# Row maxima of the fifth query tile over 320 and 320 keys instead of 512 and 128

## The chip, the cores and the metric

The kernel runs on one core of a Trainium2 chip. The metric is the device time of one execution in microseconds (us). A profile of one execution goes with it. It names the engines so: PE is TensorE's matmuls, PEld its weight loads, DVE is VectorE, ACT is ScalarE, POOL is GpSimd, SP is the queue that issues the transfers.

## What is computed

One layer of a transformer on x of shape (4, 1024, 128), in float32: causal attention with 16 heads of width 64, a residual and a layer norm, then a feed-forward part (128 to 512, a butterfly of nine stages, GELU, a second butterfly, 512 to 128), a residual and a layer norm. What the change touches is the maximum inside the softmax:

```python
q_BSHK = jnp.einsum('BSE,EHK->BSHK', x_BSE, w_q)
k_BMHK = jnp.einsum('BSE,EHK->BSHK', x_BSE, w_k)
logits_BSHM = jnp.einsum('BSHK,BMHK->BSHM', q_BSHK, k_BMHK) / math.sqrt(Kq)
mask = jnp.where(qpos >= mpos, 0.0, -jnp.inf)[None, :, None, :]
probs_BSHM = jax.nn.softmax(logits_BSHM + mask, axis=3)
```

## The kernel before

The attention runs in 32 units, one for each of 4 batches and 8 pairs of heads. The 1024 queries of a unit are 8 tiles of 128, in two chunks of 512 (`CH`; `TPC` is 4 tiles a chunk, and the index `qt == TPC` is the fifth tile). A unit has twelve steps (`STEPS`, line 47): step s takes one key tile against one chunk of queries. Chunk 0 has steps 0 to 3 and chunk 1 steps 4 to 11. Of each step `scores` (L718) makes the logits for head 0 and head 1 of the pair, two matmuls each (L727, L733), transposed, keys on the partitions, into one of two PSUM banks `SC`. ScalarE makes the exponential of each (L906) into `PR`. There are only two `SC` banks, so a half can start only when the exponential of the half two before has been made: this is the wait in L726. GpSimd masks (L534) and adds up the exponentials (L549), and the attention matmuls (L754) take them from `PR`, most of them in blocks behind steps 1, 8 and 9 (`PV_AFTER`). Before the block behind step 8 VectorE must have scaled the unit before (L1121), and for that the inverse sums must have been broadcast by a chain of DMAs (L443, L446, L449).

The exponentials are taken of logits less their row's maximum. The maxima of unit u + 1 are found while unit u runs: TensorE makes the logits once more, this time with the queries on the partitions (L666), and VectorE takes the maximum along the row. A row of query tile qt has up to (qt + 1) x 128 keys. It is cut in two parts (`keys_of`, L352). Part 0 is the first 512 keys, part 1 the rest, so the fifth tile has 512 and 128 keys. Where a part ends on the diagonal, VectorE adds the causal mask `CMASK` and takes the maximum in one custom instruction (L1034, with a short one behind it that reads the accumulator). Where it doesn't, a plain reduction does it (L1037). Each part writes its cell of `MP`.

This work is cut in groups. A group fills one of the four PSUM banks `WORK`, in turn, and its bank must have been emptied by the consumer of the group four before (`take_work`, L618). `MAXES` (line 79) is the list of the groups of maxima, 21 a unit. Groups 0 and 1 hold two tiles each. Group 6 holds two pieces of 128 keys: part 1 of the fifth tile for both heads. Groups 7 and 8 are part 0 of the fifth tile, 512 keys, one for each head. `FILL` (line 86) says by hand where each group stands in TensorE's order, for each step at three places: between the scores of head 0 and head 1, behind the scores of head 1, and late, behind the attention matmuls where there are any. ScalarE and VectorE consume in the same order. In step 5 group 6 stands between the halves, and groups 7 and 8 stand late; in step 6 groups 9 and 10 stand late, and nothing else. `FIRST_FILL` (line 133) is the same for unit 0, in which also the maxima of unit 0 itself (`FIRST`) are placed, and `PREFETCH` (line 170) is what comes ahead of it. VectorE's `window` (L1123) sets two other pieces of work behind certain groups: the low halves of the weights behind group 0, and those of the value weights behind group 6.

The other fillers are the projections of queries and keys (L637 to L639), those of the values (L647 to L649), the sums of the exponentials (L714) and the output projection (L679).

Of the kernel before, what the change touches and what calls it, by code (L numbers as in the profile page):

```python
# [28 lines left out]
P = 128  # L29
# [3 lines left out]
UNITS = B * PAIRS  # L33
TILES = S // P
CH = 512
CHUNKS = S // CH
TPC = CH // P
# [41 lines left out]
MAXES = [("max", ((h, 0, 0), (h, 1, 0))) for h in range(2)]  # L79
MAXES += [("max", ((h, qt, 0),)) for qt in range(2, TPC) for h in range(2)]  # L80
CHUNK0_MAXES = len(MAXES)
MAXES += [("max", ((0, TPC, 1), (1, TPC, 1)))]
MAXES += [("max", ((h, qt, part),)) for qt in range(TPC, TILES) for part in range(2) for h in range(2)
          if (qt, part) != (TPC, 1)]
BETWEEN, BEHIND, LATE = range(3)
FILL = [[[], [], []] for _ in range(NS)]
# [2 lines left out]
FILL[2] = [[], [("v", 0)], MAXES[1:2]]  # L89
FILL[3] = [MAXES[2:3], MAXES[3:5], []]  # L90
FILL[4] = [[], [("v", 1)] + MAXES[5:6], []]
FILL[5] = [MAXES[6:7], [], MAXES[7:9]]
FILL[6] = [[], [], MAXES[9:11]]
FILL[7] = [MAXES[11:13], [], MAXES[13:14]]
FILL[8] = [MAXES[14:15], [], MAXES[15:17]]
FILL[9] = [MAXES[17:18], MAXES[18:21], []]
FILL[10] = [[], [("proj", 0, 0)], []]
COMPOSE_AFTER = [4, 5, 9]
RECIP_AFTER = 2
# [3 lines left out]
FIRST = [("first", i) for i in range(len(MAXES))]  # L103
# [27 lines left out]


FIRST_FILL = [[[], [], []] for _ in range(NS)]
FIRST_FILL[0] = [[("proj", 1, 0)], FIRST[10:11], []]
FIRST_FILL[1] = [FIRST[11:12], FIRST[12:14], []]
FIRST_FILL[2] = [FIRST[14:15], FIRST[15:17], []]
FIRST_FILL[3] = [FIRST[17:18], FIRST[18:21], [("proj", 0, 1)] + MAXES[0:3]]
FIRST_FILL[4] = [[("proj", 1, 1)], [], MAXES[3:5]]
FIRST_FILL[5] = [MAXES[5:6], [("v", 0)] + MAXES[6:7], MAXES[7:9]]
FIRST_FILL[6] = [[], [("v", 1)], MAXES[9:11]]  # L140
FIRST_FILL[7:] = FILL[7:]
FIRST_FILLERS = [(s, place, f) for s in range(NS) for place in range(3) for f in FIRST_FILL[s][place]]
assert sorted(f for _, _, f in FIRST_FILLERS if f[0] != "first") == sorted(f for _, _, f in FILLERS if f[0] != "norm")
# [24 lines left out]


PREFETCH = [("proj", 0, 0), ("proj", 1, 0), ("v", 0), ("proj", 0, 1), ("proj", 1, 1)] + MAXES[:CHUNK0_MAXES]  # L170
PREFETCH += FIRST[CHUNK0_MAXES:10] + [("v", 1), ("proj", 0, 0)]
SCHEDULE, NUMBER, n = [], {}, len(PREFETCH)
for u in range(UNITS):
    SCHEDULE.append([])
# [36 lines left out]
def post_norm_layer(nc, x, w_q, w_k, w_v, w_o, W_exp, b_exp, up_w, up_b, down_w, W_con, b_con, down_b, out):  # L211
    ctx = ExitStack()
    with ctx:
# [137 lines left out]

        def keys_of(part, qt):  # L352

            lo = part * CH
            return lo, min(CH, (qt + 1) * P - lo)

        def ones_sums(unit, qc):

# [248 lines left out]
        def _(pe):  # L607
# [20 lines left out]
            def filler(u, f, at):  # L628
# [21 lines left out]
                elif f[0] in ("max", "first"):  # L650
# [13 lines left out]
                    for h, qt, part in pieces:  # L664
                        lo, n = keys_of(part, qt)
                        t = nc.tensor.matmul(w[:, at_col:at_col + n], QH[:, nxt, h, qt * P:(qt + 1) * P],  # L666
                                             KHL[:, nxt, h, lo:lo + n], start=True, stop=True)
                        at_col += n
# [293 lines left out]
        def _(dve):  # L962
# [8 lines left out]
            def lo(dst, src, hi_part):  # L971
                return nc.vector.tensor_tensor(dst, src, hi_part.bitcast(F32), ALU.subtract)  # L972
# [11 lines left out]
            def stage_low(unit):  # L984

                col = unit % PAIRS * P
                dve.wait_ge(weights_hi, unit + 1)
                lo(WST[:, 1, :, :], WQKV[:, 0:2, col:col + P], WST[:, 0, :, :]).then_inc(weights_lo, 1)

            def stage_v_low(unit):  # L990

                col = unit % PAIRS * P
                dve.wait_ge(v_weights_hi, unit // 2 + 1)
                lo(WSV[:, 1, :], WQKV[:, 2, col:col + 2 * P], WSV[:, 0, :]).then_inc(v_weights_lo, 1)
# [8 lines left out]
            def consume(u, f, at):  # L1003
# [19 lines left out]
                elif f[0] in ("max", "first"):  # L1023
# [3 lines left out]
                    for h, qt, part in pieces:  # L1027
                        _, n = keys_of(part, qt)
                        cell = MP[:, h * TILES + qt, part:part + 1]
                        cols = w[:, at_col:at_col + n]  # L1030
                        at_col += n
                        if (part + 1) * TPC > qt:

                            op = nc.vector.tensor_tensor_reduce(cols, cols, CMASK[:, CH - n:], 1.0, LOWEST,  # L1034
                                                                ALU.add, ALU.max, cell)
                        else:
                            op = nc.vector.tensor_reduce(cell, cols, AX_X, ALU.max)  # L1037
# [64 lines left out]
            def normalise_tile(t, done):  # L1102

                nc.vector.tensor_scalar(X[:, t, :], X[:, t, :], MV[:, t, 0:1], RSTD[:, t:t + 1],
                                        ALU.subtract, ALU.mult).then_inc(done, 1)
# [6 lines left out]
            def recip(unit):  # L1112

                dve.wait_ge(sums_landed, unit * 16 + 32)
                nc.vector.reciprocal(RCOL[:, 1, :], RCOL[:, 0, :]).then_inc(recip_made, 1)

            def scale(unit):

                dve.wait_ge(inverse_landed, unit * 32 + 32)
                for qc in range(CHUNKS):  # L1120
                    nc.vector.tensor_tensor(attended(unit, qc), O[qc][:, :], R[:, qc, :], ALU.mult).then_inc(o_free, 1)  # L1121

            def window(u):  # L1123

                for s in range(NS):
                    if (u, s) == W1_SPLIT_AT:
                        dve.wait_ge(w1_hi, 1)
                        lo(W1L, W1[:, :], W1H).then_inc(w1_lo, 1)
                    for at, _, f, n in SCHEDULE[u]:
                        if at != s:  # L1130
                            continue
                        if f[0] != "v" and f[0] != "norm":
                            consume(u, f, n)
                        if f == MAXES[0 if u > 0 else 5] and u + 2 < UNITS:
                            stage_low(u + 2)
                        if f == MAXES[6 if u > 0 else 11] and u % 2 == 0 and u + 2 < UNITS:
                            stage_v_low(u + 2)
                    if s == (RECIP_AFTER if u < UNITS - 1 else LAST_RECIP) and u > 0:
                        recip(u - 1)
                    if s == (SCALE_AFTER if u < UNITS - 1 else LAST_SCALE) and u > 0:  # L1140
                        scale(u - 1)
                    for t, when in NORMALISE_AT.items():
                        if when == (u, s):
                            dve.wait_ge(rstd_made, t // TILES + 1)
                            normalise_tile(t, x1_made)
# [13 lines left out]
            for u in range(UNITS):  # L1159
                window(u)  # L1160
# [73 lines left out]
```

## Time and profile before

| | us |
|---|---|
| median of 3 runs | 1035.61 (1035.3 to 1035.62) |
| profiled execution | 1034.01 |
| its span | 1032.3 |
| TensorE busy | 1007.2 |
| GpSimd busy | 750.5 |
| VectorE busy | 777.4 |
| ScalarE busy | 613.7 |

The span goes from the first to the last instruction of the profiled execution. An engine is busy while an instruction of it executes, waiting and issuing don't count. Matmuls overlap in TensorE's pipeline, so a matmul's listed duration is longer than its distance to the next one. In the chain of work that ended last each piece is shown with the time by which it moves the end, which for matmuls is that distance. Its start times differ by some tenths from those of the timeline, because it counts a matmul from the end of the one before.

### The profile page before, as it was taken

How to read it: one execution, taken by the hardware profiler on the slowest of the kernel's cores; microseconds unless marked ns; L12 is line 12 of the kernel's file. 1: busy time of each engine (PE TensorE's matmuls, PEld its weight loads, DVE VectorE, ACT ScalarE, POOL GpSimd, SP SyncE). 2: the span in 40 equal slices, each digit the busy share in tenths (PEclk: the TensorE clock that was granted, in tenths of full speed). 3: DMA queues.
4: the chain of work that ended last, by engine and by line, in shares of the span. 5: the costliest groups of instructions: out<-in, count | busy, mean ns of one | idle time of the engine just before them, and what ended most of it. 6: DMA issues, size and time to landing. Idle time of an engine off the chain costs nothing.

```text
span 1032.3 us, 17783 instructions
## 1 busy us (share of the span) xinstructions
PE 1007.2 (98%) x5832; PEld 698.5 (68%) x5832; DVE 777.4 (75%) x2117; ACT 613.7 (59%) x1246; POOL 750.5 (73%) x715
## 2 busy tenths in 40 slices
PE   7899999999999999999999999999999999999997
PEld 5566676676766676676666766667666766765697
DVE  7867777777777777877788787877778788775456
ACT  4555665566655656666556656666656556665544
POOL 5767888777778887777778887777778887777510
PEclk9999999999999999999999999999999999999999
DMA  5332222233222222232222222332222222320002
GB/s 154 99 99 67 53 69 57 52 83 84 63 63 62 65 70 55 63 83 64 74 72 62 61 54 54 83 83 63 64 62 71 65 56 60 84 63 22 22 11 72
DMA packets 48602, 68.71 MB, mean 67 GB/s; under 512 B 15191, under 2 KB 25083, under 8 KB 48510
## 3 DMA queue, kind: packets, MB, share of 16 engines
q1 hardware_dynamic: 48510, 67.57, 25.4%
q8 instruction: 47, 0.77, 0.3%
q14 instruction: 45, 0.37, 0.1%
HBM read 31.11 MB, written 2.36 MB: 32 GB/s over the span
## 4 chain that ended last, share of the span: by engine, by line
PE 92%; DVE 3%; DMA 2%; ACT 1%; issue 1%; SPq 0%; POOL 0%; POOLq 0%; ACTq 0%
PE O L754 25%; PE WORK L666 14%; PE SC L727 13%; PE SC L733 13%; PE WORK L679 6%; PE WORK L714 3%; PE WORK L639 3%; PE WORK L638 3%; PE WORK L637 3%; PE WORK L815 2%; PE WORK L647 1%; PE WORK L648 1%; PE WORK L649 1%; DVE WORK L1034 1%; DMA R<-RROW 1%
## 5 line engine op out<-in xcount | busy, mean ns | idle before, releaser
L906 ACT ACTIVATE PR<-SC 128x512 f32<-128x512 f32 (+3 forms) x768 | 352.6, 490 | 267.9 <-PE SC L733 242.0
L549 POOL TENSOR_TENSOR SUM<-SUM,PR 128x1024 f32<-128x1024 f32 (+3 forms) x256 | 419.3, 1638 | 14.9 <-ACT PR L906 1.0
L1034 DVE CUSTOM_DVE_ANT_0 WORK<-WORK,CMASK 128x128 f32<-128x128 f32 (+3 forms) x512 | 239.5, 514 | 64.7 <-PE WORK L666 64.6
L727 PE MATMUL SC<-QH,KHL 128*128 128x512 f32 (+3 forms) x768 | 269.2, 356 | 4.2 <-ACT PR L906 4.0
L733 PE MATMUL SC<-QL,KH 128*128 128x512 f32 (+3 forms) x768 | 261.6, 346 | 2.8 <-DMA QL<-NROW 2.8
L534 POOL TENSOR_SCALAR_AFFINE_SELECT PR<-PR 128x256 f32<-128x256 f32 x256 | 105.7, 414 | 192.3 <-ACT PR L906 192.2
L666 PE MATMUL WORK<-KHL,QH 128*128 128x512 f32 (+3 forms) x768 | 224.8, 359 | 2.3 <-DMA KH<-KHL 1.6
L754 PE MATMUL O<-PR,VLO 128*64 128x512 f32 (+3 forms) x1024 | 199.9, 522 | 1.8 <-DVE OT L1121 1.8
L727 PEld LDWEIGHTS SC<-QH,KHL 128*128 128x128 f32 x768 | 145.2, 189 | 62.7 <-ACT PR L906 30.5
L666 PEld LDWEIGHTS WORK<-KHL,QH 128*128 128x128 f32 x768 | 135.4, 189 | 54.0 <-issue 32.6
L1037 DVE TENSOR_REDUCE MP<-WORK 128x1 f32<-128x512 f32 x256 | 164.3, 684 | 4.9
L733 PEld LDWEIGHTS SC<-QL,KH 128*128 128x128 f32 x768 | 145.4, 189 | 13.7 <-DMA QL<-NROW 3.1
L972 DVE TENSOR_TENSOR QL<-WORK,QH 64x512 fp32r<-64x512 f32 x128 | 88.0, 688 | 87.1 <-ACT QH L840 85.9
L558 POOL TENSOR_TENSOR SUM<-PR 128x768 f32<-128x768 f32 x64 | 135.9, 2124 | 1.5 <-ACT PR L906 1.5
L754 PEld LDWEIGHTS O<-PR,VLO 128*64 128x64 f32 x1024 | 64.9, 136 | 106.0 <-issue 78.1
L972 DVE TENSOR_TENSOR KHL<-WORK,KHL 64x512 fp32r<-64x512 f32 x128 | 88.2, 689 | 32.9 <-ACT KHL L840 30.9
L840 ACT ACTIVATE QH<-WORK 64x512 fp32r<-64x512 f32 (+1 forms) x132 | 78.0, 591 | 15.3 <-PE WORK L639 11.5
L840 ACT ACTIVATE KHL<-WORK 64x512 fp32r<-64x512 f32 x128 | 75.8, 592 | 4.1 <-PE WORK L639 0.5
L754 PE MATMUL O<-PR,VHI 128*64 128x256 f32 (+3 forms) x512 | 74.4, 432 | 0.0
L1034 DVE DVE_READ_ACCUMULATOR2_ANT MP<- 128x1 f32 x512 | 72.6, 142 | 0.0
L754 PEld LDWEIGHTS O<-PR,VHI 128*64 128x64 f32 x512 | 36.8, 137 | 52.6 <-issue 46.3
L679 PE MATMUL WORK<-WOT,OT 128*128 128x128 f32 x512 | 63.7, 278 | 0.0
(134 smaller groups left out, 1103.7 us busy)
## 6 DMA issues: line engine op xcount, KB each, us to landing
QH<-QH SPq DMA_DIRECT2D x128, 128.0 KB, 2.3
KH<-KHL SPq DMA_DIRECT2D x128, 128.0 KB, 2.3
R<-RROW SPq DMA_DIRECT2D x64, 256.0 KB, 3.9
SW<-in_L_ffn_up_weights_dram SPq DMA_DIRECT2D x9, 512.0 KB, 4.4
SW<-_L_ffn_down_weights_dram SPq DMA_DIRECT2D x9, 512.0 KB, 4.4
out_dram<-X SPq DMA_DIRECT2D x7, 256.0 KB, 2.3
X<-in_L_attn_x_BSE_dram SPq DMA_DIRECT2D x3, 512.0 KB, 4.4
X<-in_L_attn_x_BSE_dram SPq DMA_DIRECT2D x2, 256.0 KB, 2.9
```

The source lines that it names most:

```text
L549: nc.gpsimd.tensor_tensor(total, total, prob(unit, s), ALU.add).then_inc(add_done, 1)
L558: nc.gpsimd.tensor_tensor(total, first[:, :, START[s]:], prob(unit, s), ALU.add).then_inc(add_done, 1)
L666: t = nc.tensor.matmul(w[:, at_col:at_col + n], QH[:, nxt, h, qt * P:(qt + 1) * P], KHL[:, nxt, h, lo:lo + n], start=True, stop=True)
L679: t = nc.tensor.matmul(w[:, k * P:(k + 1) * P], attended(pair, qc)[:, k * P:(k + 1) * P], WOT[:, pair % PAIRS, :], start=pair < last, stop ...
L727: nc.tensor.matmul(dst, KHL[:, par, h, kt * P:(kt + 1) * P], QH[:, par, h, q0:q0 + n], start=True, stop=False)
L733: nc.tensor.matmul(dst, KH1[:, par, h, kt * P:(kt + 1) * P], QL[:, par, h, q0:q0 + n], start=False, stop=True).then_inc(scores_ready, 1)
L754: t = nc.tensor.matmul(O[qc][h * K:(h + 1) * K, START[s]:], values(unit, kt)[:, h * K:(h + 1) * K], p[:, h, :], start=kt == 0, stop=s == L ...
L840: return nc.scalar.activation(dst, src, ACT.Copy)
L906: nc.scalar.activation(prob(unit, s)[:, h, :], SC[use % NSC][:, 0:n], ACT.Exp, scale=K ** -0.5).then_inc(exp_done, 1)
L972: return nc.vector.tensor_tensor(dst, src, hi_part.bitcast(F32), ALU.subtract)
L1034: op = nc.vector.tensor_tensor_reduce(cols, cols, CMASK[:, CH - n:], 1.0, LOWEST, ALU.add, ALU.max, cell)
L1037: op = nc.vector.tensor_reduce(cell, cols, AX_X, ALU.max)
```

## The change

`keys_of` cuts the fifth tile in two parts of 320 keys. Group 6, with the two pieces of 128 keys, becomes two groups of one piece of 320 keys each. That makes 22 groups a unit, and all numbers behind it go up by one in the three hand-written orders. The two new groups stand where the one stood, between the halves of step 5 (in unit 0 behind step 5's scores). The two groups with part 0 stay late in step 5, with 320 keys each. The 128 columns on the diagonal lie at the end of part 1, and `CMASK` is taken from its end, so the same instruction masks them. The low halves of the value weights stay behind group 6, which is now the first of the two new ones.

```diff
-MAXES += [("max", ((0, TPC, 1), (1, TPC, 1)))]
+MAXES += [("max", ((h, TPC, 1),)) for h in range(2)]
...
-FILL[5] = [MAXES[6:7], [], MAXES[7:9]]
-FILL[6] = [[], [], MAXES[9:11]]
-FILL[7] = [MAXES[11:13], [], MAXES[13:14]]
-FILL[8] = [MAXES[14:15], [], MAXES[15:17]]
-FILL[9] = [MAXES[17:18], MAXES[18:21], []]
+FILL[5] = [MAXES[6:8], [], MAXES[8:10]]
+FILL[6] = [[], [], MAXES[10:12]]
+FILL[7] = [MAXES[12:14], [], MAXES[14:15]]
+FILL[8] = [MAXES[15:16], [], MAXES[16:18]]
+FILL[9] = [MAXES[18:19], MAXES[19:22], []]
...
-FIRST_FILL[5] = [MAXES[5:6], [("v", 0)] + MAXES[6:7], MAXES[7:9]]
-FIRST_FILL[6] = [[], [("v", 1)], MAXES[9:11]]
+FIRST_FILL[5] = [MAXES[5:6], [("v", 0)] + MAXES[6:8], MAXES[8:10]]
+FIRST_FILL[6] = [[], [("v", 1)], MAXES[10:12]]
...
-PREFETCH += FIRST[CHUNK0_MAXES:10] + [("v", 1), ("proj", 0, 0)]
+PREFETCH += FIRST[CHUNK0_MAXES:11] + [("v", 1), ("proj", 0, 0)]
...
-            lo = part * CH
-            return lo, min(CH, (qt + 1) * P - lo)
+            size = (TPC + 1) * P // 2 if qt == TPC else CH
+            lo = part * size
+            return lo, min(size, (qt + 1) * P - lo)
...
-                        if f == MAXES[6 if u > 0 else 11] and u % 2 == 0 and u + 2 < UNITS:
+                        if f == MAXES[6 if u > 0 else 12] and u % 2 == 0 and u + 2 < UNITS:
```

## Rows read from the trace of the kernel before

**Rows 1.** The page: busy time of the engines, and the chain by engine.
```profile
PE 1007.2 (98%) x5832; PEld 698.5 (68%) x5832; DVE 777.4 (75%) x2117; ACT 613.7 (59%) x1246; POOL 750.5 (73%) x715
...
PE 92%; DVE 3%; DMA 2%; ACT 1%; issue 1%; SPq 0%; POOL 0%; POOLq 0%; ACTq 0%
```

**Rows 2.** Chain that ended last, 482 to 490 us: start, us it moves the end, what.
```profile
483.43 0.12 PE WORK L648
...
484.72 0.17 PE WORK L666 x2
484.90 0.28 PE SC L727
485.18 0.23 PE SC L733
485.41 0.47 PE WORK L666 x2
...
486.34 0.26 PE SC L727
```

**Rows 3.** The same chain, 491.5 to 502: 384 columns first, the others 128.
```profile
493.50 0.18 PE SC L733
...
498.47 0.06 PE SC L727
498.53 0.11 PE SC L733
...
498.86 1.84 PE WORK L679 x16
```

**Rows 4.** Timeline around step 6 of unit 15: start, us, instruction, [idle before, releaser].
```profile
485.02 0.39 PE L733 MATMUL SC<-QL,KH 128*128 128x512 f32 x1
...
485.45 0.60 ACT L906 ACTIVATE PR<-SC 128x512 f32<-128x512 f32 x1
...
486.10 0.19 PEld L727 LDWEIGHTS SC<-QH,KHL 128*128 128x128 f32 x1 [0.19 <-ACT PR L906]
...
486.44 0.39 PE L733 MATMUL SC<-QL,KH 128*128 128x512 f32 x1
```

**Rows 5.** Timeline of the last unit, which has no maxima, 949.9 to 950.8 us.
```profile
949.28 1.11 ACT L906 ACTIVATE PR<-SC 128x512 f32<-128x512 f32 x2
...
950.44 0.19 PEld L727 LDWEIGHTS SC<-QH,KHL 128*128 128x128 f32 x1 [0.19 <-ACT PR L906]
...
950.78 0.40 PE L733 MATMUL SC<-QL,KH 128*128 128x512 f32 x1
```

**Rows 6.** VectorE's groups by shape: busy us, mean ns of one, idle before.
```profile
L1037 DVE TENSOR_REDUCE MP<-WORK 128x1 f32<-128x512 f32 x256 | 164.3, 684 | 4.9
...
L1034 DVE CUSTOM_DVE_ANT_0 WORK<-WORK,CMASK 128x256 f32<-128x256 f32 x128 | 55.6, 455 | 0.0
...
L1034 DVE CUSTOM_DVE_ANT_0 WORK<-WORK,CMASK 128x128 f32<-128x128 f32 x128 | 37.2, 311 | 31.5 <-PE WORK L666 31.5
```

**Rows 7.** Timeline of VectorE and TensorE, unit 15, from the late groups to step 8.
```profile
485.68 2.71 DVE L1037 TENSOR_REDUCE MP<-WORK 128x1 f32<-128x512 f32 x4
...
488.43 1.29 DVE L1121 TENSOR_TENSOR OT<-O,R 128x512 f32<-128x512 f32 x2
...
489.80 0.65 PE L754 MATMUL O<-PR,VLO 128*64 128x512 f32 x2
```

**Rows 8.** Waits: who waited for whom, us in total, times, longest.
```profile
DVE OT L1121 <- DMA R<-RROW: 14.7, 15, 6.2
...
PE SC L733 <- DMA QL<-NROW: 2.8, 1, 2.8
...
PE O L754 <- DVE OT L1121: 1.8, 2, 1.0
...
PE WORK L647 <- DVE MP L1034: 1.4, 1, 1.4
```

**Rows 9.** Stretch by engine: busy us (instructions) of PE, PEld, DVE, ACT, POOL; clock; DMA.
```profile
38.30:41.70 3.40, 3.40 (x10) 2.62 (x10) 1.45 (x4) 2.63 (x6) 3.04 (x4) 0.53 0.23 52
```

More of the change, by code:

```diff
@@ L133 @@
 FIRST_FILL = [[[], [], []] for _ in range(NS)]
[L134 to L137, printed above, removed]
+FIRST_FILL[0] = [[("proj", 1, 0)], FIRST[11:12], []]
+FIRST_FILL[1] = [FIRST[12:13], FIRST[13:15], []]
+FIRST_FILL[2] = [FIRST[15:16], FIRST[16:18], []]
+FIRST_FILL[3] = [FIRST[18:19], FIRST[19:22], [("proj", 0, 1)] + MAXES[0:3]]
 FIRST_FILL[4] = [[("proj", 1, 1)], [], MAXES[3:5]]
-FIRST_FILL[5] = [MAXES[5:6], [("v", 0)] + MAXES[6:7], MAXES[7:9]]
-FIRST_FILL[6] = [[], [("v", 1)], MAXES[9:11]]
+FIRST_FILL[5] = [MAXES[5:6], [("v", 0)] + MAXES[6:8], MAXES[8:10]]
+FIRST_FILL[6] = [[], [("v", 1)], MAXES[10:12]]
 FIRST_FILL[7:] = FILL[7:]
```

## The prediction

> **What bounds the kernel now.** I read the page first: TensorE is busy 98% of the span and the chain that ended last is TensorE for 92% [rows 1]. So only what TensorE must do, or must wait for, counts. Next comes the chain of work in one ordinary unit, from 482 to 490 us [rows 2]: its second column is how far one matmul moves the end, which is the price to use, since the durations of the timeline overlap (a 512-column matmul is listed at 0.39 us [rows 4] and moves the chain by 0.23). Units 1 to 30 repeat this piece; unit 31 has no maxima, and unit 0 is start-up. In it stand, one behind the other: scores of step 5 head 0, the group of two 128-column matmuls ("x2, 0.17"), scores of step 5 head 1 (0.28 + 0.23), the two 512-column groups placed late in step 5 (0.47), scores of step 6 head 0, and scores of step 6 head 1, whose first matmul takes 0.26 and not 0.23 [rows 2]. That 0.26 is the second thing to see: at this place TensorE is already just waiting for ScalarE.
>
> **The change, part by part.** Of a unit's 24 matmuls for row maxima four change: 128, 128 and 512, 512 columns become 320 four times. The columns are 1280 in both.
>
> Prices. 512 columns move the chain by 0.23, 256 by 0.12 [rows 2], so 64 columns are 0.0275, and 384 should be 0.175 (the row prints 0.18 [rows 3]). 320 columns lie between: 0.1475. Below 256 the line breaks: sixteen 128-column matmuls, each with weights of its own, take 1.84, or 0.115 each [rows 3], as much as 256 columns. The pair in step 5 shows the same when its debt is counted: 0.17 for the pair and 0.28 - 0.23 = 0.05 by which the next matmul is late, 0.22 together [rows 2].
>
> (a) The group between the halves of step 5 becomes two groups of 320: 0.295 for 0.22, so +0.075. Bounds for the 320: not below the 256's 0.12 (+0.02 for the pair) and not above the 384's 0.175 (+0.13); I take the line between them.
>
> (b) The two late groups become 2 x 0.1475 = 0.295 for 0.47, so -0.17 of TensorE's work. If only work counted, (a) and (b) would give -0.095 a unit, -3 us in all.
>
> (c) But the late groups are cover for a wait. A score bank is free when the exponential of the half two before has read it. Follow step 5 head 1 [rows 4]: its second matmul starts at 485.02, the exponential at 485.45, it takes 0.60 and ends at 486.05; the weight load of step 6 head 1, which had been waiting, starts at 486.10, and that half's second matmul at 486.44, 0.39 behind the exponential's end. From 485.02 to 486.44 are 1.42 us that the late groups have no part in. What TensorE must issue in the same time is six matmuls of 0.23: 1.38, or 1.39 with the late pair at its 0.47. It is the shorter of the two already now, by the 0.03 seen as 0.26. With (b) it would be 1.22, and the floor stays 1.42. That 0.39 behind the exponential is a floor, and not simply the time at which TensorE happened to arrive, is shown by the last unit, where nothing fills in between: exponentials end at 949.28 + 1.11 = 950.39, the load that waited starts at 950.44, the second matmul at 950.78, again 0.39 [rows 5]. So all of (b) turns into waiting there, and (a), which stands ahead of step 5 head 1 and moves the start of its exponential, is paid in full. Step 6 head 0 needs only the exponential of step 5 head 0, which is done well before, and gains nothing for the end. From step 6 head 1 on all is as before, 0.075 later.
>
> (d) VectorE. The 128-column masked maxima (0.311) become 320: from 455 for 256 and 1.1 ns a column, about 0.53, +0.22 each; the plain maxima of 512 (0.684) lose 192 columns, about -0.2 each [rows 6]. The sum is near zero, and it is done before the groups of step 6: at present its four plain maxima run from 485.68 to 488.39, the third and fourth of them on step 6's groups, and the scaling starts at 488.43 [rows 7]. The first scaling, which the attention matmuls of step 8 need, is over by 489.1, while these start only at 489.80 [rows 7]: over half a microsecond of cover. In even units the subtraction for the value weights, until now behind the short pair, comes to stand between the two new groups; it is the same work, and TensorE doesn't wait for it there. If that cover were gone, the attention matmuls would start later by what exceeds it.
>
> (e) One more group. Its wait is on a bank used four groups earlier; consecutive groups in the chain follow at 0.23, so a wait that is met costs nothing [rows 2]. The rotation moves by one for the next four groups: the first 320 of the late pair now takes the bank of the value projection, which ScalarE copies out ahead of step 5's exponentials. No wait. In the start-up VectorE is behind, though: the second value projection already waits 1.4 us for it [rows 8], and its bank will be that of the second new group, not of the short pair, released 2 x 0.22 later. Bounds 0 and +0.4; less the 0.09 that unit 0 may gain at the place where it waits for a copy and not for ScalarE. I take +0.1.
>
> (f) Given back. VectorE waits 15 times for the broadcast of the inverse sums before it scales, and twice, 1.8 us together, TensorE waits with it [rows 8]. Those transfers start in step 1, ahead of the change, so in such a unit the 0.075 is free. With units that are near it: -0.2.
>
> Sum: 30 x 0.075 = 2.25, + 0.1, - 0.2 = **+2.15 us**. The profiled execution has a span of 1032.3 and took 1034.0; it would take 1036.2. The median of the runs, 1035.6, lies 1.6 above it and should move alike: 1037.7.
>
> **A rule weighed.** The chain has 0.115 for each of the sixteen 128-column matmuls [rows 3]. The Trainium skill, page "TensorE: Matmul & The Clock Gate", section "Back-to-back issue gap", gives for a stream of weight load and matmul about 81 ns at 128 columns and 131 at 512. By its 81 ns the pair would be 0.16 and (a) 0.135, and the sum about +4.0 us. The trace disagrees with both of its figures, and the measurement decides.
>
> **The rivals.**
> A, faster: the wait of (c) isn't a floor, because ScalarE takes up the earlier start. Then work alone counts: 32 sets x -0.095 = -3.0, 1032.6. For it speaks the page's 98%; against it the 0.26 and the last unit's 0.39. It decides if exponentials of step 5 could start earlier, and they start when the scores are there.
> B, nothing: the broadcast of the inverse sums lands late in most units of the timed runs, so TensorE waits for it anyway; the 1.6 us between the profiled execution and the median may be such waits. +0.3 or less, 1035.8. Against it: only two TensorE waits in the trace [rows 8].
> C, slower: the pair of 128s has no debt, and the 0.28 behind it is a cost of the score matmul that stays. Then the pair cost 0.17, as where a 128-column matmul follows at 0.06 and the next at 0.11 [rows 3]; (a) is 0.125, 30 times: +3.8, 1039.3. By the sixteen in a row that is unlikely.
> D: the clock. At 38.3 to 41.7 us the granted clock is 0.53, so the 1.2 GHz level for nearly all of it, with ten matmuls in 3.4 us [rows 9], behind a wait of 2.8 us in unit 0 for the row of maxima [rows 8]. A start-up shifted by tenths could keep or lose it: -1.5 or +1.5.
>
> **How the numbers follow.** The forecast case has 0.70, A 0.08, B 0.09, C 0.09, D 0.04, half each way. A measurement of this kernel can tell about 0.2%, 2.1 us, from no change, and the forecast of +2.1 lies on that line: its 0.70 goes half to "within", half to "slower". Faster: 0.08 + 0.02 = 0.10. Within: 0.35 + 0.09 = 0.44. Slower: 0.35 + 0.09 + 0.02 = 0.46. The forecast's own range is +1.0 to +3.2 (the 320's price between 0.13 and 0.16, start-up and late landings). For 8 in 10 it is widened to B below and into C above: 1035.2 to 1039.0; A is left out.
>
> **What the changed profile would show.** In the chain of an ordinary unit: two matmuls of line 666 at about 0.15 each and a score matmul of 0.23 where 0.28 stood; late in step 5 "x2" at about 0.30; and in front of step 6 head 1 a wait of about 0.17 for the exponential, in the rows of TensorE's waits for line 906, some 30 of them. TensorE's busy time falls by some 3 us while the span grows by about 2. If the span shrinks and the wait isn't there, (c) is wrong; if the wait is there and the score matmul keeps 0.28, C; if line 754 waits for VectorE in many units, (d) or B.

## The result and the profile after

The changed kernel takes 1038.4 us (median of 8 runs, 1036.5 to 1039.6) where the kernel before takes 1035.5 in the same runs (8, 1034.2 to 1036.4). The ratio is 1.0031, with an interval of 1.0021 to 1.0040: slower by 3.2 us by the ratio, 2.9 by the two medians. Timed once more beside the experiments it had 1.0029 (1.0018 to 1.0041). The profiled execution took 1039.4 and is near the slowest of its runs, while that of the kernel before, 1034.0, was faster than all eight of its own. So the two profiles differ by 5.3 us of span, more than the kernels do, and the start is kept apart from the units in what follows.

The page of the changed kernel, the lines that answer to [rows 1]. Lines behind `keys_of` are numbered one higher than before, so 666 is now 667, and 727 is 728:

```profile
span 1037.6 us, 17783 instructions
...
PE 1011.3 (97%) x5832; PEld 701.5 (68%) x5832; DVE 772.5 (74%) x2117; ACT 617.5 (60%) x1246; POOL 750.7 (72%) x715
```

The chain of unit 15, which answers to [rows 2] (start, us by which it moves the end, what; it is the same unit as there, a few us later):

```profile
488.26 0.23 PE SC L728
488.49 0.23 PE SC L734
488.72 0.29 PE WORK L667 x2
489.01 0.23 PE SC L728
489.24 0.23 PE SC L734
489.48 0.29 PE WORK L667 x2
489.77 0.23 PE SC L728
489.99 0.23 PE SC L734
490.23 0.44 PE SC L728
490.67 0.23 PE SC L734
```

From the top: scores of step 5 head 0; the two new groups, 0.29 where the pair of 128s had 0.17 and left the next matmul 0.05 late; that matmul, now at 0.23; the late pair, 0.29 for 0.47; scores of step 6 head 0; and the first matmul of step 6 head 1, which takes 0.44. It took 0.26 before and would take 0.23 if nothing held it. What the late pair no longer costs, 0.18, stands again at this matmul. The timeline says what holds it, and answers to [rows 4]; the other matmuls are left out:

```profile
489.08 0.40 PE L734 MATMUL SC<-QL,KH 128*128 128x512 f32 x1
...
489.52 1.35 ACT L907 ACTIVATE PR<-SC 128x512 f32<-128x512 f32 x2 [0.16 <-PE SC L734]
...
490.17 0.19 PEld L728 LDWEIGHTS SC<-QH,KHL 128*128 128x128 f32 x1 [0.37 <-ACT PR L907]
...
490.51 0.39 PE L734 MATMUL SC<-QL,KH 128*128 128x512 f32 x1
```

The exponential of step 5 head 1 starts at 489.52 and takes 0.60, to 490.12 (the row joins it with the next). The load starts 0.05 behind its end and the second matmul 0.39 behind its end, the same distances as in [rows 4] and [rows 5]. From the second matmul of step 5 head 1 to that of step 6 head 1 are 1.43 us; before they were 1.42.

How much a unit costs is read over 29 of them, from the first score matmul of step 4 of unit 1 to that of unit 30. Kernel before, then after:

```profile
72.46 0.47 PE L727 MATMUL SC<-QH,KHL 128*128 128x512 f32 x1
```
```profile
919.82 0.40 PE L727 MATMUL SC<-QH,KHL 128*128 128x512 f32 x1
```
```profile
75.19 0.47 PE L728 MATMUL SC<-QH,KHL 128*128 128x512 f32 x1
```
```profile
924.89 0.40 PE L728 MATMUL SC<-QH,KHL 128*128 128x512 f32 x1
```

The units take 847.36 and 849.70 us: +2.34, or 0.081 each. In both, about 2.0 of it are waits of TensorE for scalings that a late broadcast held up. They are counted by how much later than usual the first attention matmul of a block comes, so they are a little above the 1.8 and 2.0 that the rows of waits have. What comes behind unit 30 differs by 0.3. The rest of the profiles' difference, 2.7 us, arose ahead of that first point of unit 1. The waits and the clock of the start-up are looked at with the runs on it.

### The profile page after: what moved, and what is told of

It reads as the page before. It is cut to its first block, busy times and chain, and to the rows that moved or that the text cites. A ratio compares the mean times of both kernels' runs of the same rounds, so it can differ in the third digit from the quotient of the medians.

```text
span 1037.6 us, 17783 instructions
## 1 busy us (share of the span) xinstructions
PE 1011.3 (97%) x5832; PEld 701.5 (68%) x5832; DVE 772.5 (74%) x2117; ACT 617.5 (60%) x1246; POOL 750.7 (72%) x715
## 3 DMA queue, kind: packets, MB, share of 16 engines
q1 hardware_dynamic: 48510, 67.57, 25.3%
## 4 chain that ended last, share of the span: by engine, by line
PE 90%; DMA 4%; DVE 3%; ACT 2%; issue 1%; SPq 0%; POOL 0%; ACTq 0%; POOLq 0%
PE O L755 25%; PE WORK L667 13%; PE SC L728 13%; PE SC L734 12%; PE WORK L680 5%; PE WORK L715 3%; PE WORK L638 3%; PE WORK L640 3%; PE WORK L639 3%; PE WORK L816 2%; DMA R<-RROW 2%; PE WORK L648 1%; PE WORK L650 1%; PE WORK L649 1%; DVE WORK L1035 1%; DMA RROW<-RCOL 1%
## 5 line engine op out<-in xcount | busy, mean ns | idle before, releaser
L907 ACT ACTIVATE PR<-SC 128x512 f32<-128x512 f32 (+3 forms) x768 | 356.2, 490 | 266.2 <-PE SC L734 238.3
L1035 DVE CUSTOM_DVE_ANT_0 WORK<-WORK,CMASK 128x384 f32<-128x384 f32 (+4 forms) x512 | 252.7, 538 | 67.6 <-PE WORK L667 67.5
L667 PE MATMUL WORK<-KHL,QH 128*128 128x512 f32 (+4 forms) x768 | 223.5, 357 | 3.3 <-DMA KH<-KHL 1.6
L728 PEld LDWEIGHTS SC<-QH,KHL 128*128 128x128 f32 x768 | 145.0, 189 | 63.3 <-ACT PR L907 31.4
L1038 DVE TENSOR_REDUCE MP<-WORK 128x1 f32<-128x512 f32 (+1 forms) x256 | 151.4, 633 | 9.8 <-PE WORK L667 9.7
```

Of the source, the lines that this page charges most:

```text
L728: nc.tensor.matmul(dst, KHL[:, par, h, kt * P:(kt + 1) * P], QH[:, par, h, q0:q0 + n], start=True, stop=False)
L907: nc.scalar.activation(prob(unit, s)[:, h, :], SC[use % NSC][:, 0:n], ACT.Exp, scale=K ** -0.5).then_inc(exp_done, 1)
```

## The experiments

All runs were timed against the kernel before, on one chip for each set of four. "Units" is the time of the 29 units in the profile, read as above; in the kernel before it is 847.4, and "start" (to step 4 of unit 1) 72.5. The column "us" is the ratio's part over 1, times the median of the kernel before in the same set. Late broadcasts put 0.3 to 2.2 us of waits into "units", differently in each execution, so a difference of one microsecond there is not yet a finding.

| kernel | ratio to before (interval) | us | units | start |
|---|---|---|---|---|
| changed kernel | 1.0031 (1.0021 to 1.0040) | +3.2 | 849.7 | 75.2 |
| changed kernel again | 1.0029 (1.0018 to 1.0041) | +3.0 | 849.1 | 73.9 |
| before, late pair 320 columns | 0.9994 (0.9985 to 1.0003) | -0.6 | 847.7 | 72.8 |
| changed, one late matmul twice | 1.0021 (1.0012 to 1.0030) | +2.2 | 848.8 | 74.0 |
| before, one late matmul twice | 1.0045 (1.0032 to 1.0058) | +4.7 | 852.1 | 72.9 |
| second new group late | 0.9989 (0.9980 to 0.9998) | -1.1 | 844.6 | 74.0 |
| three 320s and more late | 1.0059 (1.0046 to 1.0071) | +6.1 | 851.8 | 73.9 |
| start-up's maxima as before | 1.0019 (1.0010 to 1.0028) | +2.0 | 849.2 | 73.4 |
| start-up's maxima alone changed | 1.0008 (0.9999 to 1.0017) | +0.8 | 847.2 | 73.4 |
| start-up's order | 1.0031 (1.0020 to 1.0042) | +3.2 | 849.8 | 74.7 |
| start-up's order, second group late | 0.9994 (0.9985 to 1.0003) | -0.6 | 844.7 | 73.9 |
| old start, second group late | 0.9983 (0.9974 to 0.9992) | -1.8 | 844.2 | 74.2 |
| 384 and 256 keys | 0.9977 (0.9967 to 0.9987) | -2.4 | 844.5 | 73.1 |

### Is the floor real? Work taken away, and work added

The floor is the 1.42 us of the prediction's (c): the second matmul of step 6 head 1 can't come earlier than that behind the second matmul of step 5 head 1, because the exponential lies between them. The first of three runs takes work away from the kernel before and puts nothing in its place: part 0 of the fifth tile leaves out keys 320 to 511 in units 1 to 31. Only the function is shown; its calls pass `f[0] == "first"`.

```diff
-        def keys_of(part, qt):
+        def keys_of(part, qt, first):
 
             lo = part * CH
-            return lo, min(CH, (qt + 1) * P - lo)
+            n = (TPC + 1) * P // 2 if (part, qt) == (0, TPC) and not first else CH
+            return lo, min(n, (qt + 1) * P - lo)
...
```

> The kernel before with the late pair of step 5 cut to 320 columns and nothing put in its place: part 0 of the fifth tile reads only the first 320 keys, so keys 320 to 511 are left out of the fifth tile's maxima (only for units 1 to 31). 0.17 us of TensorE's work a unit is gone. Theory of the floor: TensorE then waits for the exponential of step 5 head 1, and nothing is won: within 0.5 us of the kernel before. Rival, work alone counts: -0.17 x 31 = -5.2 us.

It measured -0.6 us with an interval of -1.6 to +0.3, and units of 847.7 us for 847.4; -5.2 was what work alone would give. The chain of its profile around step 6 (start, us, what) says the same:

```profile
485.13 0.28 PE SC L728
485.41 0.23 PE SC L734
485.64 0.30 PE WORK L667 x2
485.94 0.23 PE SC L728
486.17 0.23 PE SC L734
486.40 0.43 PE SC L728
```

The late pair has 0.30 for 0.47, and the score matmul behind it 0.43 for 0.26. So 0.17 us of TensorE's work were removed from each of 31 units for nothing, on an engine that the page has busy for 98%.

The second adds 0.147 us of work at the same place in the changed kernel, the third 0.23 in the kernel before. The edit is the same in both:

```diff
-                        t = nc.tensor.matmul(w[:, at_col:at_col + n], QH[:, nxt, h, qt * P:(qt + 1) * P],
-                                             KHL[:, nxt, h, lo:lo + n], start=True, stop=True)
+                        for _ in range(2 if (f[0], h, qt, part) == ("max", 0, TPC, 0) else 1):
+                            t = nc.tensor.matmul(w[:, at_col:at_col + n], QH[:, nxt, h, qt * P:(qt + 1) * P],
+                                                 KHL[:, nxt, h, lo:lo + n], start=True, stop=True)
```

> The changed kernel with one matmul of the late pair of step 5 (fifth tile, part 0, head 0, 320 columns) issued twice, for each of 31 units; the result is the same. Theory of the floor: TensorE waits there about 0.17 to 0.2 us a unit for the exponential of step 5 head 1, so 0.147 us more of work disappears in the wait: the time of the changed kernel within 0.4 us (+3.2 us against the kernel before), and the wait ahead of step 6 head 1 shrinks. Rival, work alone counts: +0.147 x 31 = +4.6 us on top, +7.8 us against the kernel before.

It measured +2.2, not above the changed kernel's +3.0 and far from +7.8. Its chain has the three matmuls at 0.43 and the waiting one at 0.30 instead of 0.44:

```profile
487.95 0.43 PE WORK L668 x3
488.38 0.23 PE SC L729
488.61 0.23 PE SC L735
488.84 0.30 PE SC L729
```

> Control on the kernel before: one matmul of its late pair of step 5 (fifth tile, part 0, head 0, 512 columns) issued twice for each of 31 units. Theory of the floor: before the change TensorE's own work there is only 0.03 us under the floor, so of the 0.23 us nearly all is paid: 0.20 x 31 = +6.2 us against the kernel before, where the same doubling in the changed kernel cost nothing. Rival, that a doubled matmul on a bank is hidden or cheap in itself: under +2 us.

It measured +4.7 us, less than the 6.2 expected (its interval is +3.3 to +6.0) and far above 2. Here the whole matmul is added to the chain, 0.69 for 0.47, and the wait behind it is gone, 0.23 for 0.26:

```profile
488.03 0.69 PE WORK L667 x3
488.73 0.23 PE SC L728
488.96 0.23 PE SC L734
489.19 0.23 PE SC L728
```

Its units take 852.1 us, +4.8, with only 0.3 us of waits for late scalings where the kernel before had 2.0. Without those waits a unit is 0.226 longer (29.375 for 29.149), nearly the whole 0.23 of the doubled matmul. Most likely the delay in each unit also gave late broadcasts more time, but no run changed that alone. So the same doubling is free in the one kernel and paid in the other. The difference between them is the cover that the change removed.

### Cover put back

```diff
-FILL[5] = [MAXES[6:8], [], MAXES[8:10]]
+FILL[5] = [MAXES[6:7], [], MAXES[7:10]]
```

> The changed kernel with the second of the two new groups (fifth tile, part 1, head 1) moved from between the halves of step 5 to the late place of step 5, ahead of the late pair. Same work, same instructions. Theory of the floor: ahead of step 5 head 1 stand 0.147 us in place of 0.295 (before the change 0.22), and the late place has 0.44 us, which fits under the floor of 1.42 us; an ordinary unit is 0.147 us shorter than in the changed kernel and 0.073 shorter than before: 30 x 0.073 = -2.2 us against the kernel before for the units, and with the start-up's loss of about 1 us, -1.2 us. Rival, work alone counts: no difference from the changed kernel, +3.2 us.

-1.1 us against the kernel before (interval -2.1 to -0.2), so about 4 below the changed kernel, with the same instructions; units of 844.6 us, -2.7, of which 0.8 are fewer waits for scalings. Without these a unit is 0.067 shorter than in the kernel before. The chain:

```profile
485.14 0.15 PE WORK L667
485.28 0.23 PE SC L728
485.52 0.23 PE SC L734
485.75 0.44 PE WORK L667 x3
486.19 0.23 PE SC L728
486.42 0.24 PE SC L734
486.65 0.28 PE SC L728
```

The chain has 0.15 ahead of step 5 head 1, 0.44 late, and a wait of only 0.05 left. The place of one group decides the sign of the change.

The next went further and moved the group ahead as well, so that 0.59 us stand late. (It has also the start-up's order of the run told of below.)

```diff
-FILL[4] = [[], [("v", 1)] + MAXES[5:6], []]
-FILL[5] = [MAXES[6:8], [], MAXES[8:10]]
+FILL[4] = [[], [("v", 1)], []]
+FILL[5] = [MAXES[5:6], [], MAXES[6:10]]
```

> As the run before it, and the group ahead of the new ones (fourth tile, head 1, 512 columns) moved from behind the scores of step 4 to between the halves of step 5, with both new groups late. Then 0.59 us of groups stand late in step 5, and what TensorE must issue between the second matmuls of step 5 head 1 and step 6 head 1 is 1.51 us, more than the floor of 1.42, so no wait is left there. Theory: 2.43 us from the scores of step 5 on in place of 2.49, so 0.057 x 30 = -1.7 us on top, -3.9 us against the kernel before: the whole of the 0.1 us of work that the change saves, and the 0.03 that was waited before. Rival, that VectorE, which gets this group 0.2 us later, holds up the attention matmuls of step 8: no gain on top, -2.2 us or worse.

It measured +6.1 us: worse than all others. The rival had VectorE holding up the attention matmuls of step 8. It was VectorE, but at a place that neither theory nor rival had named. The chain has the four late matmuls at 0.80, not 0.59, and the score matmuls behind at 0.23 and 0.24, so the wait for the exponential is gone and another stands in its place. The timeline of its weight loads and of VectorE shows which:

```profile
488.50 0.70 DVE L1035 CUSTOM_DVE_ANT_0 WORK<-WORK,CMASK 128x512 f32<-128x512 f32 x1 [0.75 <-PE WORK L667]
...
489.11 0.14 DVE L1035 DVE_READ_ACCUMULATOR2_ANT MP<- 128x1 f32 x1
...
489.31 0.19 PEld L667 LDWEIGHTS WORK<-KHL,QH 128*128 128x128 f32 x1 [0.21 <-DVE MP L1035]
```

The fourth of the late groups needs the bank of the group four before, which is now the 512-column one between the halves. VectorE ends it at 489.25, and the load comes at 489.31, 0.21 late. Here five groups within one step are more than the four banks carry. In all, such waits of the loads of line 667 are 13.5 us in this kernel, 51 times, and 4.7, 11 times, in the changed one. This explains the larger part, not all: 0.21 a unit, less the 0.057 that was to be won, would be 4.6 us above the run before it, and 6.7 were measured.

### The start-up

```diff
+OLD = [("max", ((h, 0, 0), (h, 1, 0))) for h in range(2)]
+OLD += [("max", ((h, qt, 0),)) for qt in range(2, TPC) for h in range(2)]
+OLD += [("max", ((0, TPC, 1), (1, TPC, 1)))]
...
-FIRST = [("first", i) for i in range(len(MAXES))]
+FIRST = [("first", i) for i in range(len(OLD))]
...
-            size = (TPC + 1) * P // 2 if qt == TPC else CH
+            size = (TPC + 1) * P // 2 if qt == TPC and not first else CH
```

> The change for the maxima that are found while a unit runs (31 sets), but the maxima of unit 0 itself, which the start-up makes, cut in 512 and 128 as before. Theory of the two parts: an ordinary unit costs 0.075 us more (the two 320-column groups ahead of the exponential of step 5 head 1), 30 times, so about +2.2 us against the kernel before; the start-up, which in the two traces differs by 2 to 2.7 us, goes back to what it was. Rival, that the start-up's difference is chance of one execution: the same time as the changed kernel, +3.2 us.

> The other half alone: only the maxima of unit 0 itself are cut in 320 and 320, in the start-up; all later units as before. Theory: one more group in the start-up puts the 512-column group behind it on a bank that VectorE hasn't emptied, so TensorE waits longer; +0.5 to +2.7 us against the kernel before, the more the more often the clock falls to its lower level there. Rival, that the start-up is no part of the loss: within 0.3 us of the kernel before.

The diff is of the first; the second has the old list and the old columns for the units' own groups, and the new ones where `first` is set. They measured +2.0 and +0.8 us, together 2.8 and near the +3.0 of the changed kernel; the interval of the second (-0.1 to +1.8) just holds zero, so that this share exists is likely and not shown by the times alone. The first was to have the start of the kernel before; its profiled start is 73.4, as late as that of the second. Two places are seen in the profiles, and one belongs to each run. This is TensorE's timeline of the changed kernel at its waits:

```profile
21.95 0.80 PE L667 MATMUL WORK<-KHL,QH 128*128 128x512 f32 x1 [1.38 <-DVE MP L1035]
22.54 0.49 PE L648 MATMUL WORK<-WSV,XTH 128*128 128x256 f32 x1
...
48.57 0.38 PE L648 MATMUL WORK<-WSV,XTH 128*128 128x256 f32 x1 [0.84 <-DVE MP L1035]
```

and this the kernel before at the same places:

```profile
21.71 0.35 PE L647 MATMUL WORK<-WSV,XTH 128*128 128x256 f32 x1 [1.43 <-DVE MP L1034]
...
46.24 1.04 PE L666 MATMUL WORK<-KHL,QH 128*128 128x512 f32 x2 [0.34 <-DVE MP L1034]
```

With one group more, a 512-column group stands ahead of the second value projection and waits for VectorE as the projection did. Then the projection comes, at 22.54, 0.83 later; 0.24 of that arose earlier, at a wait for the copies of the keys. This place belongs to the second run, whose profile has the same wait, 1.38. The other one is in unit 0. There the second value projection had the bank of the first, which ScalarE empties; now it has that of a new group, and waits 0.84 for VectorE where the next group had waited 0.34. This place belongs to the first run, which waits 0.88 there.

Of the 2.7 us by which the two profiled starts differ, about 1.4 are there in the second execution of the changed kernel too. The other 1.3 are for the most part the clock. In the first execution it fell to the 1.2 GHz level (0.50) from 21.9 to 25.3 us as well, when TensorE had waited 1.38; the same kernel run again had the same wait and no fall. Rows by stretch (PE, PEld, DVE, ACT, POOL busy, clock, DMA), first the changed kernel, then the same again:

```profile
22.00:25.30 3.30, 3.30 (x11) 2.79 (x12) 1.68 (x5) 0.60 (x1) 0.00 (x0) 0.50 0.49 163
```
```profile
22.00:25.30 3.30, 3.17 (x16) 2.55 (x17) 1.83 (x6) 1.56 (x3) 0.00 (x0) 1.00 0.46 126
```

11 matmuls are in the first stretch and 16 in the second. The one start took to 75.2 us, the other to 73.9, the kernel before 72.5. In the timed runs the clock is no large part of the loss. Beside the repeat the mean granted clock is 0.9963 for the kernel before (25 runs) and 0.9963 for the changed one (6). In the set of the two start-up runs it is 0.9968 before and 0.9964 and 0.9963 for them. One fall of 3.4 us to half takes 0.0016 of the mean, so by these numbers they have about 0.3 falls more a run; that is an estimate.

The next run puts the 512-column group behind the projection again:

```diff
-FIRST_FILL[0] = [[("proj", 1, 0)], FIRST[11:12], []]
+FIRST_FILL[0] = [[("proj", 1, 0)], FIRST[10:12], []]
...
-PREFETCH += FIRST[CHUNK0_MAXES:11] + [("v", 1), ("proj", 0, 0)]
+PREFETCH += FIRST[CHUNK0_MAXES:10] + [("v", 1), ("proj", 0, 0)]
```

> The changed kernel with one edit in the start-up: the 512-column group that follows the four groups of the fifth tile (sixth tile, head 0) goes behind the second value projection again, into step 0 of unit 0, instead of ahead of it. Theory: the start-up's loss of about 1 us comes from this group, which waits for a bank that VectorE empties late, with the value projection queued behind it; without it the loss of the units alone is left, about +2.1 us against the kernel before. Rival, that the cut in 320 and 320 itself costs in the start-up: still about +3 us.

It measured +3.2: the edit that was to mend the start gave nothing. Its profiled start was 74.7 us, with three falls of the clock, the first of them behind a wait of 2.06 us for the copies of the keys, which no edit touches. The same order with the second group late:

> The start-up's order as in the run before it, and the second new group late in step 5. Theory: the units give -0.073 x 30 = -2.2 us against the kernel before, and the start-up nothing: -2.2 us. Rival, that the start-up's order is worth nothing: -1.3 us, as with the late group alone.

It measured -0.6 us, above the -2.2 expected and nearer to its rival of -1.3. The units agree, 844.7, as with the late group alone. The start is no better, 73.9, with one fall of the clock. So the falls of the run before don't hide a gain, and this profile shows where it goes. The scores of unit 0 begin 0.13 us behind the kernel before, where with the old order and the late group they begin 0.67 behind. But then a 512-column group behind step 1 waits for VectorE, which it doesn't in the old order:

```profile
28.63 0.50 PE L667 MATMUL WORK<-KHL,QH 128*128 128x512 f32 x1 [0.34 <-DVE MP L1038]
```

So the scores of step 2 begin 0.85 behind instead of 0.68, and from step 7 on both are 1.5 behind. The order moves the wait and doesn't remove it.

### A version that is faster than both

Both of these have the start-up's own maxima as before and the second new group late. In unit 0 the group 9 of the list goes behind the second value projection, so that three groups stand between the two projections, and the second has again the bank of the first. In unit 0 the first of the two kernels still shows a group that waits 0.76 us for VectorE, and its profiled start is 74.2, so it is the late group that carries the gain. The first four lines of the diff are in both kernels. The last two, against the first kernel, are in the second alone:

```diff
-FIRST_FILL[5] = [MAXES[5:6], [("v", 0)] + MAXES[6:8], MAXES[8:10]]
-FIRST_FILL[6] = [[], [("v", 1)], MAXES[10:12]]
+FIRST_FILL[5] = [MAXES[5:6], [("v", 0)] + MAXES[6:7], MAXES[7:9]]
+FIRST_FILL[6] = [[], [("v", 1)], MAXES[9:12]]
...
-            size = (TPC + 1) * P // 2 if qt == TPC and not first else CH
+            size = 3 * P if qt == TPC and not first else CH
```

> 320 and 320 keys in the units with the second new group late in step 5, the maxima of unit 0 itself cut as before, and in unit 0 three groups behind the second value projection in place of four ahead of it, so that its bank is again one that ScalarE empties. Theory: the units give -0.067 us each, as the profile of the run with the late group has it, 30 times -2.0, and the start-up is that of the kernel before: -2.0 us against it. Rival, that the start-up's loss is chance: -1.3 us, as that run.

> As the run before it, but the fifth tile is cut in 384 and 256 keys: 256 columns move the chain by 0.12 and 384 by 0.175. Ahead of step 5 head 1 stands one group of 0.12, and late in step 5 stand 0.12 + 2 x 0.175 = 0.47, as much as before the change, so the late place still covers the wait up to the 0.03. Theory: 0.22 - 0.12 = 0.10 us a unit against the kernel before, 30 times -3.0 us. Rival, that only the count of columns matters: no difference from the run before it, -2.0 us.

They measured -1.8 and -2.4 us against the kernel before, and neither interval holds zero; that the second is better than the first isn't shown, the intervals overlap, and the rival of -2.0 for the second stands. In the profiles its unit isn't shorter either: without the waits for scalings it is 29.07 us, and 29.06 in the first. The chain of the second has 0.12 ahead of step 5 head 1 and 0.47 late, and the wait at 0.03, as before the change:

```profile
483.77 0.12 PE WORK L672
...
484.35 0.47 PE WORK L672 x3
484.82 0.23 PE SC L733
485.05 0.24 PE SC L739
485.29 0.26 PE SC L733
```

> The changed kernel once more, beside the others. All theories: +3.2 us against the kernel before, within its interval of +2.2 to +4.1; it tells how often its start-up falls to the lower clock: with one such stretch, as in the kernel before, +2.8 us, with two, +5.

This is the repeat whose numbers stand above: +3.0, and one fall of the clock in its profile.

## Why the prediction was right, and where it wasn't

Forecast were +2.1 us, with the line between "within" and "slower" running through it; +3.2 and +3.0 were measured, in the range, at the upper end of the forecast's own +1.0 to +3.2, and slower by more than 0.2%. The mechanism was right; about a third of the measured size came from elsewhere.

(a), the price of the four matmuls, was right: 320 columns move the chain by 0.147 (0.29 for two), and the pair of 128s had cost the 0.05 behind it too. That matmul went back to 0.23, as (a) said, and rival C, by which it would have kept 0.28, fell. 0.075 a unit were forecast and 0.081 measured, 2.4 us for 2.25. By the 81 ns of the Trainium skill's page "TensorE: Matmul & The Clock Gate", section "Back-to-back issue gap", it would have been 0.135; the runs stand nearer to the rows than to the page.

(b) and (c), that the 0.17 saved late in step 5 turns into waiting, was right in place, cause and size: 1.42 us became 1.43, the load follows the exponential by 0.05 and the second matmul by 0.39. Taking the work away alone gave nothing, putting 0.147 back cost nothing, and the control on the kernel before paid. Rival A fell.

(d) held: the 320-column masked maximum takes 0.521 (0.53 forecast), the plain one 0.482 (0.684 less 0.2), and the attention matmuls wait for a scaling about as often as before: 28 waits of weight loads, 12.6 us, for 25, 11.2 us, and three of TensorE's own, 2.0 us, for two, 1.8 us. Rival B, +0.3 us or less, fell by the measured time itself.

(e) was mis-sized, and it is most likely the greater part of the missing microsecond: +0.1 for the start-up, where 0.6 to 0.8 are left of the measured +3.0 and +3.2 when the units' 2.4 are taken off, and where the run of the start-up's own maxima has +0.8 (its interval just holds zero). The sum saw that the second value projection would wait for a later bank. It didn't see that the group behind the fifth tile's now stands ahead of that projection and waits, nor that in unit 0 the bank of the value projection passes from ScalarE to VectorE, with a wait of 0.84 us. There it even booked a gain. No time shows what this second place costs: the run that has it alone measured +2.0, less than the units' 2.4. Of the 22 groups the sum followed the rotation only in the steady unit.

Rival D, the clock, came true in one of the two profiles of the changed kernel, and by the granted clocks of the timed runs it has little part in their +3.0.

(f) can't be told apart from chance: the waits of TensorE for late scalings are 2.0 us in both profiles and 0.3 to 2.2 in the others, so no run shows its 0.2 given back.

Two of the signs to look for were wrong. The waits of the loads for the exponential were to grow by some 30 times 0.17; they are 31.4 us in 108 waits now and 30.5 in 137 before, and TensorE's own waits for it are 9 for 8. A load idles ahead of every score that comes early; the waits at step 6 head 1 grew from 0.19 to 0.37 each, while those at step 7 head 0, 0.17 each, vanished, since its exponential had time. Idle time of the loads isn't time of the chain. And TensorE's busy time was to fall by 3 us; it rose by 4, from 1007.2 to 1011.3, because a matmul that waits is listed from its load on (0.50 for 0.39), and one more stretch was at the lower clock.

## What to carry to other kernels

On an engine that is busy for 98%, work can still be cover, that is, fill time in which the engine would wait anyway: find for each wait the two events whose distance is fixed (here a score matmul and the one two halves on, 1.42 us apart), sum what is issued between them, and cut work only where the sum is above the time between them, or move other work in when it falls below. Small pieces should go where the saving is paid out, and here the place of one 0.15 us group in each unit was worth 4 us. When a list gets one entry more, follow the rotation of its banks in the special first round too, not in the steady one alone, and count how many groups stand within one stretch against the number of banks.

## What was not expected of the hardware

The granted clock of TensorE fell to its lower level (1.2 GHz) in the start-up of all 14 profiled executions, around the wait of 2.5 to 2.8 us for the row of maxima: from 0.6 us ahead of the wait's end to 1.5 us behind it. In three of them it also fell elsewhere. Twelve have a wait of about 1.4 us that ends at 22 us, and it fell at one of them, in one of two executions of the same kernel. It fell behind both waits of 2.1 us for the copies of the keys. In the run of the start-up's order it fell a third time at 30.7 us, where the last waits had been of 0.97, 0.52 and 0.34 us.

What a fall costs can be read from one pair alone, the two executions of the changed kernel. By the first scores of unit 0 they are 1.05 us apart, 0.15 of it from before the fall, and at step 4 of unit 1 they are 1.3 apart. The other two pairs with different numbers of falls, 74.7 and 73.9 (start-up's order) and 74.2 and 73.1 (the two kernels faster than both), don't show it: 1.1 and 0.75 us of their difference had arisen before, at a longer wait for the copies of the keys.

A doubled matmul added 0.226 us to each unit of the kernel before, which would be 7.0 us in 31 units. The total rose by 4.7, with an interval that ends at 6.0. In its profile the waits for late broadcasts are 0.3 us instead of 2.0.
